# Attention kernel: projections in two halves after the scores, and the transposed maximum ahead of the last weighted values

## The chip, the cores and the metric

The kernel runs on one core of a Trainium2 chip. A core has TensorE (PE, matrix products; its weight loads are listed as PEld), VectorE (DVE), ScalarE (ACT), GpSimd (POOL) and SyncE (SP, which here only issues transfers). The metric is the time of one execution on the device in microseconds (us), the median of several runs.

## The reference, cut to what matters

32 batches of 128 tokens of width 128 go through cross attention with 16 heads and through a mixture of 8 experts of which each token takes 2.

```python
x = x + tanh(g_xattn[0]) * xattn(layernorm(x), ctx_1024, ctx_1024, ...)
x = x + tanh(g_ffn[0]) * ffn(layernorm(x), ...)

# xattn, with q the normalised x and k = v = the context
q, k = apply_rope(q), apply_rope(k)
Q, K, V = (split_heads(t @ W.T + b) for t, W, b in ...)     # 16 heads of 8
scores = einsum('bhqd,bhkd->bhqk', Q, K) / sqrt(8)
out = einsum('bhqk,bhkd->bhqd', softmax(scores), V)
return merge_heads(out) @ Wo_w.T + Wo_b

# ffn
xn = rms_norm(x, norm_scale)
c, ids = top-2 of softmax(xn @ w_router.T)
val, gate = split(xn @ w_up[e])                             # hidden width 352
out = sum over the two experts of c * ((val * silu(gate)) @ w_down[e]) + x
```

## The kernel before, in words

The program is written engine by engine: five instruction streams in fixed order, tied by semaphores that are counted. No scheduler moves anything, so an instruction runs when those ahead of it on its engine have gone and its semaphores have been reached. The attention part fills about 31 to 257 us of the profile, the expert part the rest.

The attention loop has one step a batch, b = 0 to 31. Four batches are a chunk c = b // 4, u = b % 4 is the place in it, and four steps are a period. Within step b TensorE does, for batch b, the scores by key (`scores_by_key`, L1348, four groups into the two banks STB), and the weighted values (`weighted_values`, L1361, four groups); for batch b+2, the scores by query (`scores`, L1335, four groups into the two banks SB); for batch b-1, the transposes of the heads (`heads_by_query`, L1388), of the attended rows (`transpose_attended`, L1399) and the output projection (`project_out`, L1403 and L1404). What softmax subtracts is found two steps ahead: DVE takes the maximum of each group of scores by query (`maximum`, L840, four a step), TensorE transposes them (`transpose_maximum`, L1393), and DVE writes them as a high part and a low part (`maximum_high` L847, `maximum_low` L851), which SP's transfers put below the stacked queries for `scores_by_key` of that batch. The transposed maximum lies in the bank of the second group of scores, so this group (L1335, g=1) of the next step waits until L851 has read it. ACT takes the exponent of each group of scores by key (L573), and copies the values' sums (`heads_out`, L580), the attended rows (L586) and others out of the banks.

On top of this each step does a part of what a whole chunk needs. In u=0: the V projection of chunk c+1 (L1321), the positions of routed rows (L1432 to L1435), on DVE the choice of experts and `shift` (L798). In u=1: the transposes of x (L1287) and of the context (L1295) for chunk c+2, their copies on ACT (L540, L547) and the rotation of Q on DVE (L806). In u=2: `project_q` (L1303, L1304) into the bank PR; ACT takes its high part in bf16 (`high`, L554), DVE the remainder (`remainder`, L832), ACT a middle part (L560), POOL the lowest; and `transpose_rows` (L1414) for the router of chunk c-1. In u=3: `project_k` (L1313, L1314) with the same parts, the router (L1423), and on ACT `base` (L602, four activations). Both projections, the V projection and all those transposes use the one bank PR in turn. POOL sends the routed rows out by indirect transfers (L427). SP's queue carries the stacked parts of Q and K (six pieces each a chunk), the maxima and the loads. Chunks 6 and 7 have no Q and K projection any more.

## Time and profile before

| | |
|---|---|
| median of 3 runs | 470.53 us (468.91 to 471.07) |
| the profiled execution | 470.41 us, its span 468.6 us |
| mean granted clock of TensorE | 0.917 of full speed |
| PE / DVE / ACT / POOL busy | 411.8 / 301.8 / 261.7 / 242.7 us |
| steps 12 to 15 (one period), 111.75 to 140.48 us | 28.73 us, PE busy 25.03 |

The profiled execution is 1.8 us longer than its span, since the span counts from the first to the last recorded instruction. A busy PE means matmuls in flight; their ends are modelled. What an engine waits for stands in brackets behind its row in the timeline, with the line that released it.

### The profile page before, as it was taken

How to read it: one execution, taken by the hardware profiler on the slowest of the kernel's cores; microseconds unless marked ns; L12 is line 12 of the kernel's file. 1: busy time of each engine (PE TensorE's matmuls, PEld its weight loads, DVE VectorE, ACT ScalarE, POOL GpSimd, SP SyncE). 2: the span in 40 equal slices, each digit the busy share in tenths (PEclk: the TensorE clock that was granted, in tenths of full speed). 3: DMA queues.
4: the chain of work that ended last, by engine and by line, in shares of the span. 5: the costliest groups of instructions: out<-in, count | busy, mean ns of one | idle time of the engine just before them, and what ended most of it. 6: DMA issues, size and time to landing. Idle time of an engine off the chain costs nothing.

```text
span 468.6 us, 13323 instructions
## 1 busy us (share of the span) xinstructions
PE 411.8 (88%) x3821; PEld 278.8 (59%) x3824; DVE 301.8 (64%) x1167; ACT 261.7 (56%) x582; POOL 242.7 (52%) x201
## 2 busy tenths in 40 slices
PE   7988899988898898989898939996799998999991
PEld 3445465645555466555555627674577876777871
DVE  6877888987878677777884414563655554555550
ACT  3437586977777676666665415752255554555540
POOL 6090242365446454454333475568466537886663
PEclk9998999999998897996956778998899999999997
DMA  7714341446579224232011322444334423344330
GB/s 185 177 47 126 75 112 35 121 135 173 145 206 232 63 65 115 77 88 79 30 43 48 87 52 43 68 59 94 59 48 61 58 47 49 56 57 56 37 28 0
DMA packets 57422, 39.07 MB, mean 83 GB/s; under 512 B 8819, under 2 KB 55158, under 8 KB 57366
## 3 DMA queue, kind: packets, MB, share of 16 engines
q1 hardware_dynamic: 43622, 28.87, 23.9%
q0 software_dynamic: 12736, 8.64, 13.1%
q10 hardware_dynamic: 1008, 0.85, 0.8%
q8 instruction: 30, 0.49, 0.5%
q14 instruction: 26, 0.21, 0.2%
HBM read 14.26 MB, written 11.75 MB: 56 GB/s over the span
## 4 chain that ended last, share of the span: by engine, by line
PE 61%; DVE 15%; issue 7%; ACT 5%; DMA 5%; another core or an unknown queue 4%; POOLq 1%; POOL 0%; DVEq 0%; ACTq 0%
PE bank L1595 9%; PE bank L1573 8%; PE bank L1575 7%; PE bank L1361 5%; DVE nmx L840 5%; PE bank L1585 4%; DMA out<-ys,yi 4%; PE bank L1388 3%; PE bank L1393 3%; PE bank L1335 3%; PE bank L1348 2%; PE bank L1303 2%; ACT pt L573 2%; PE bank L1304 2%
## 5 line engine op out<-in xcount | busy, mean ns | idle before, releaser
L509 POOL DMA_INDIRECT out<-ys,yi x72 | 112.6, 1564 | 63.8 <-issue 35.3
L427 POOL DMA_INDIRECT slots_dram<-xr,slu x64 | 62.7, 979 | 68.9 <-ACT pt L573 55.3
L840 DVE TENSOR_REDUCE nmx<-bank 128x4 f32<-128x512 f32 x128 | 81.8, 681 | 5.9 <-PE bank L1335 5.7
L1595 PEld LDWEIGHTS bank<-wf_sb,hT 128*128 128x128 f32 (+1 forms) x432 | 58.6, 197 | 39.0 <-issue 35.2
L1595 PE MATMUL bank<-wf_sb,hT 128*128 (+1 forms) x432 | 63.7, 285 | 19.9 <-DVE hT L1203 15.4
L573 ACT ACTIVATE pt<-bank 128x512 f32<-128x512 f32 x128 | 72.5, 594 | 14.6 <-PE bank L1348 12.8
L1193 DVE TENSOR_TENSOR hh<-sg,bank 128x352 f32<-128x352 f32 x72 | 37.5, 520 | 53.5 <-ACT sg L707 28.4
L715 ACT ACTIVATE ys<-bank,yc 128x128 f32<-128x128 f32 x72 | 26.5, 368 | 76.6 <-PE bank L1595 32.0
L1573 PE MATMUL bank<-wf_sb,xT 128*128 x144 | 58.1, 487 | 0.1
L1361 PE MATMUL bank<-pt,v 128*9 128x128 f32 x1024 | 53.7, 296 | 3.5 <-ACT pt L573 2.5
L1575 PE MATMUL bank<-wf_sb,xT 128*128 x144 | 55.9, 470 | 0.0
L1202 DVE COPY hT<-bank 128x256 f32<-128x256 f32 x72 | 30.5, 424 | 38.5 <-PE bank L1585 17.8
L1335 PE MATMUL bank<-ks,qs 62*128 62x128 bf16 x512 | 40.4, 229 | 8.4 <-DVE mTs L851 5.7
L707 ACT ACTIVATE sg<-bank 128x352 f32<-128x352 f32 x72 | 33.4, 464 | 17.2 <-PE bank L1573 10.3
L1575 PEld LDWEIGHTS bank<-wf_sb,xT 128*128 128x128 f32 x144 | 28.6, 199 | 16.6 <-issue 2.4
L1585 PE MATMUL bank<-con,hh 128*128 128x128 f32 (+1 forms) x216 | 36.6, 279 | 0.0
L1335 PEld LDWEIGHTS bank<-ks,qs 62*128 62x128 bf16 x512 | 28.0, 100 | 13.6 <-issue 9.2
L1361 PEld LDWEIGHTS bank<-pt,v 128*9 128x9 f32 x1024 | 16.7, 90 | 31.1 <-issue 17.4
L699 ACT ACTIVATE xT<-bank,ns_sb 128x128 f32<-128x128 f32 x72 | 26.4, 367 | 15.3 <-PE bank L1565 8.6
L1348 PE MATMUL bank<-qs,ks 64*128 64x128 bf16 x512 | 28.8, 235 | 0.0
L1388 PE MATMUL bank<-con,oT 128*128 128x128 f32 x128 | 24.8, 325 | 3.7 <-ACT oT L580 2.1
L408 POOL TENSOR_TENSOR parts<-r,parts 128x512 bf16<-128x512 f32 x14 | 16.2, 1161 | 22.5 <-ACT parts L560 22.3
(191 smaller groups left out, 699.9 us busy)
## 6 DMA issues: line engine op xcount, KB each, us to landing
qs<-parts SPq DMA_DIRECT2D x48, 128.0 KB
ks<-parts SPq DMA_DIRECT2D x45, 128.0 KB
xs<-slots_dram SPq DMA_DIRECT2D x72, 66.0 KB
wf_sb<-in_wup SPq DMA_DIRECT2D x8, 352.0 KB
x_sb<-in_x SPq DMA_DIRECT2D x8, 256.0 KB, 3.5
ctx_sb<-in_ctx_in SPq DMA_DIRECT2D x8, 256.0 KB, 3.7
out<-x_sb SPq DMA_DIRECT2D x8, 256.0 KB, 2.4
out<-ys,yi POOLq DMA_INDIRECT x72
```

The lines of the kernel that those rows point to most:

```text
L427: nc.gpsimd.indirect_dma_start(out=slots_dram, out_offset=bass.IndirectOffsetOnAxis(ap=slu[:, c % 2, k, kk:kk + 1], axis=0), in_=xr[:, c % ...
L509: nc.gpsimd.indirect_dma_start(out=out.rearrange("b s d -> (b s) d"), out_offset=bass.IndirectOffsetOnAxis(ap=yi[:, r:r + 1], axis=0), in_ ...
L573: nc.scalar.activation(pt[:, 4 * g:4 * g + 4, :], STB[g % 2][:, :].rearrange("p (h s) -> p h s", h=4), ACT.Exp, scale=SCORE_SCALE).then_in ...
L840: nc.vector.tensor_reduce(nmx[:, b % 2, at:at + 4], SB[g % 2][:, :].rearrange("p (h s) -> p h s", h=4), AX.X, ALU.max, negate=True).then_i ...
L1335: last = mm(SB[g % 2][:, k * S:(k + 1) * S], qs[row:row + ROWS, c % NST, i, t0:t0 + S], ks[row:row + ROWS, c % NST, i, t0:t0 + S], start=T ...
L1348: last = mm(STB[g % 2][:, k * S:(k + 1) * S], ks[row:row + 64, c % NST, i, t0:t0 + S], qs[row:row + 64, c % NST, i, t0:t0 + S], start=True ...
L1361: last = mm(PVB[32 * k:32 * k + DK + 1, g * S:(g + 1) * S], v9[:, c % 2, b % CH, 4 * g + k, :], pt[:, 4 * g + k, :], start=True, stop=True)
L1388: last = nc.tensor.transpose(HB[:, g * S:(g + 1) * S], oT[:, g, :], ident)
L1573: mm(bank[2 * (r % 2)][:, 0:H], xT[:, r % 2, :], wf_sb[:, bass.ds(w + H, H)], start=True, stop=True)\
L1575: mm(bank[2 * (r % 2) + 1][:, 0:H], xT[:, r % 2, :], wf_sb[:, bass.ds(w, H)], start=True, stop=True)\
L1585: last = nc.tensor.transpose(bank[5][0:w, 128 * n:128 * n + 128], hh[:, r % 2, 128 * n:128 * n + w], ident)
L1595: last = mm(Y[:, 0:D], hT[0:wide, r % 2, 128 * n:128 * n + 128], wf_sb[0:wide, bass.ds(w + 2 * H + n * D, D)], start=(n == 0), stop=(n == ...
```

## The change

Nothing is computed otherwise, and no instruction is added or dropped apart from waits. (1) TensorE: the projections of Q and K are cut into their two matmuls, which go behind the last scores of the step, with `transpose_attended` between them; this one and they come ahead of the second group of weighted values. (2) TensorE: `transpose_maximum` goes ahead of the third and fourth groups of weighted values, and ahead of the row transposes, the router and the context transposes. (3) ACT: the high part of Q goes from ahead of the third exponent to behind the fourth, that of K to the end of the step behind `base`. (4) DVE: the remainders go behind the transposed maximum's two parts; `shift` goes behind the choice of experts; `variance` goes between the third and fourth maximum and `widen` ahead of the parts. (5) The row transposes of chunks 0 to 5 use the bank HB in place of PR, with waits to match. The diff, cut to its core:

```diff
@@ act @@
-                if u == 2 and there(c + 2):
-                    high(c + 2, 0, PR)
-                if u == 3 and there(c + 2):
-                    high(c + 2, 1, PR)
...
                     rows(c - 1, (2, 3))
+                if u == 2 and there(c + 2):
+                    high(c + 2, 0, PR)
                 if u == 2 and there(c - 1) and c < NCH - 1:
                     rows_transposed(c - 1)
...
                 if u == 3 and there(c - 1):
                     base(c - 1)
+                if u == 3 and there(c + 2):
+                    high(c + 2, 1, PR)
@@ dve @@
-                if u == 0 and there(c + 2) and c:
-                    shift(c + 2)
...
-                if u == 2 and there(c + 2):
-                    remainder(c + 2, 0, PR)
-                if u == 3 and there(c + 2):
-                    remainder(c + 2, 1, PR)
...
                     choose_sum(c - 2)
+                if u == 0 and there(c + 2) and c:
+                    shift(c + 2)
                 if real(b + 2):
                     maximum(b + 2, 2)
+                if u == 3 and there(c + 3):
+                    variance(c + 3)
                 if real(b + 2):
                     maximum(b + 2, 3)
...
                 if u == 3 and there(c + 3):
-                    variance(c + 3)
+                    widen(c + 3)
                 if real(b + 2):
                     maximum_high(b + 2)
                     maximum_low(b + 2)
+                if u == 2 and there(c + 2):
+                    remainder(c + 2, 0, PR)
+                if u == 3 and there(c + 2):
+                    remainder(c + 2, 1, PR)
@@ pe @@
-            def project_q(n, ps):
+            def project_q(n, ps, half):
 
-                pe.wait_ge(d_q, n + 1)
-                if n >= 2:
-                    pe.wait_ge(a_cT, n + 1)
-                mm(ps[:, :], wqk_sb[:, 0, :], qa[:, :], start=True, stop=False)
-                mm(ps[:, :], wqk_sb[:, 1, :], qb[:, :], start=False, stop=True).then_inc(pe_q, 1)
+                if half == 0:
+                    pe.wait_ge(d_q, n + 1)
+                    if n >= 2:
+                        pe.wait_ge(a_cT, n + 1)
+                    mm(ps[:, :], wqk_sb[:, 0, :], qa[:, :], start=True, stop=False)
+                else:
+                    mm(ps[:, :], wqk_sb[:, 1, :], qb[:, :], start=False, stop=True).then_inc(pe_q, 1)
...
@@ heads_by_query @@
+                if u == 2 and there(c - 1) and c < NCH - 1:
+                    pe.wait_ge(a_nT, c)
@@ transpose_rows @@
-                if c == NCH - 1:
-                    pe.wait_ge(d_tp, c)
-                pe.wait_ge(d_rq, min(c + 4, NCH))
-                pe.wait_ge(d_rk, min(c + 3, NCH))
-                pe.wait_ge(a_v, min(c + 3, NCH))
+                if c == NCH - 2:
+                    pe.wait_ge(a_v, NCH)
+                else:
+                    pe.wait_ge(d_on, min(b, B))
+                    if c:
+                        pe.wait_ge(d_tp, c)
@@ the loop of pe @@
-                if u == 2 and there(c + 2):
-                    project_q(c + 2, PR)
-                if u == 3 and there(c + 2):
-                    project_k(c + 2, PR)
...
                     scores(b + 2, 3)
+                if u == 2 and there(c + 2):
+                    project_q(c + 2, PR, 0)
+                if u == 3 and there(c + 2):
+                    project_k(c + 2, PR, 0)
+                if real(b - 1):
+                    transpose_attended(b - 1)
+                if u == 2 and there(c + 2):
+                    project_q(c + 2, PR, 1)
+                if u == 3 and there(c + 2):
+                    project_k(c + 2, PR, 1)
                 if real(b):
                     weighted_values(b, 1)
-                if real(b - 1):
-                    transpose_attended(b - 1)
...
+                if real(b + 2):
+                    transpose_maximum(b + 2)
+                if u == 2 and there(c - 1) and c < NCH - 1:
+                    transpose_rows(c - 1, b)
+                if u == 3 and there(c - 1) and c < NCH - 1:
+                    router(c - 1, b)
+                if u == 1 and there(c + 2):
+                    transposes_ctx(c + 2, PR)
...
                 if real(b):
                     weighted_values(b, 2)
                     weighted_values(b, 3)
-                if real(b + 2):
-                    transpose_maximum(b + 2)
```

TensorE in step u=3 of the second chunk, before: from the heads' transposes (out of `oT`) over the projection of K (`ka`, `kb`), the values (`pt,v`), the scores by key (`qs,ks`) and by query (`ks,qs`) and the router (`nTs`) to the transposed maximum (`nmx`) and the output projection (`onT`).

```order
132 L1388 MATMUL bank<-con,oT 128x128 x4
133 L1313 MATMUL bank<-ka,wqk_sb 128x512
134 L1314 MATMUL bank<-kb,wqk_sb 128x512
135 L1361 MATMUL bank<-pt,v 9x128 x4
136 L1348 MATMUL bank<-qs,ks 128x128 x8
137 L1335 MATMUL bank<-ks,qs 128x128 x8
138 L1361 MATMUL bank<-pt,v 9x128 x4
139 L1399 MATMUL bank<-con,on 128x128
140 L1423 MATMUL bank<-wr_sb,nTs 128x8 x4
141 L1361 MATMUL bank<-pt,v 9x128 x8
142 L1393 MATMUL bank<-con,nmx 16x128
143 L1403 MATMUL bank<-wo_sb,onT 128x128
```

The same place of TensorE in the changed kernel.

```order
133 L1392 MATMUL bank<-con,oT 128x128 x4
134 L1363 MATMUL bank<-pt,v 9x128 x4
135 L1350 MATMUL bank<-qs,ks 128x128 x8
136 L1337 MATMUL bank<-ks,qs 128x128 x8
137 L1314 MATMUL bank<-ka,wqk_sb 128x512
138 L1403 MATMUL bank<-con,on 128x128
139 L1316 MATMUL bank<-kb,wqk_sb 128x512
140 L1363 MATMUL bank<-pt,v 9x128 x4
141 L1397 MATMUL bank<-con,nmx 16x128
142 L1428 MATMUL bank<-wr_sb,nTs 128x8 x4
143 L1363 MATMUL bank<-pt,v 9x128 x8
144 L1407 MATMUL bank<-wo_sb,onT 128x128
```

The projection's two matmuls have gone behind the scores, with the attended transpose between them, and the transposed maximum has passed the router and eight value matmuls.

VectorE in the third chunk's step u=3 and on into the next, before: remainder (`r`), maxima (`nmx`), variance (`BN_AGGR`), the two parts of the transposed maximum (`mTs`), router scores (`sc`), attention added (`x_sb`), then step u=0.

```order
188 L832 SCALAR_TENSOR_TENSOR r<-bank,bqk_sb,parts 128x512
189 L840 TENSOR_REDUCE nmx<-bank 128x4 x2
190 L789 BN_AGGR mv<-st 128x2 x4
191 L847 CAST mTs<-bank 16x128
192 L851 TENSOR_TENSOR mTs<-bank,mTs 16x128
193 L903 COPY sc<-bank 128x32
194 L868 SCALAR_TENSOR_TENSOR x_sb<-bank,tg,x_sb 128x128
195 L794 TENSOR_SCALAR ve<-mv 128x4
196 L874 BN_STATS st6b<-x_sb 128x6
197 L840 TENSOR_REDUCE nmx<-bank 128x4 x2
```

VectorE in the changed kernel, at the same place.

```order
190 L840 TENSOR_REDUCE nmx<-bank 128x4
191 L789 BN_AGGR mv<-st 128x2 x4
192 L840 TENSOR_REDUCE nmx<-bank 128x4
193 L794 TENSOR_SCALAR ve<-mv 128x4
194 L847 CAST mTs<-bank 16x128
195 L851 TENSOR_TENSOR mTs<-bank,mTs 16x128
196 L832 SCALAR_TENSOR_TENSOR r<-bank,bqk_sb,parts 128x512
197 L903 COPY sc<-bank 128x32
198 L868 SCALAR_TENSOR_TENSOR x_sb<-bank,tg,x_sb 128x128
199 L874 BN_STATS st6b<-x_sb 128x6
```

The remainder now stands behind both parts of the transposed maximum, and the variance between two maxima.

ScalarE in the fifth chunk's step u=3 and the start of the next, before: exponents (`pt`), the K high part (`parts<-bank`), attended rows (`onT`), the middle part (`parts<-r`), base rows (`x_sb`) and the heads' copy (`oT`).

```order
170 L573 ACTIVATE pt<-bank 128x512 x2
171 L554 ACTIVATE parts<-bank,bqk_sb 128x512
172 L573 ACTIVATE pt<-bank 128x512
173 L586 ACTIVATE onT<-bank 128x128
174 L573 ACTIVATE pt<-bank 128x512
175 L560 ACTIVATE parts<-r 128x512
176 L602 ACTIVATE x_sb<-x_sb,fbias,fscale 128x128 x4
177 L580 ACTIVATE oT<-bank 128x512
```

ScalarE at the same place in the changed kernel.

```order
165 L573 ACTIVATE pt<-bank 128x512 x3
166 L586 ACTIVATE onT<-bank 128x128
167 L573 ACTIVATE pt<-bank 128x512
168 L560 ACTIVATE parts<-r 128x512
169 L602 ACTIVATE x_sb<-x_sb,fbias,fscale 128x128 x4
170 L554 ACTIVATE parts<-bank,bqk_sb 128x512
171 L580 ACTIVATE oT<-bank 128x512
```

The K high part has moved from behind the second exponent to the end of the step, between the base rows and the next step's copy of the heads.

## Rows read from the trace of the kernel before

**Rows 1.** The page: granted clock of TensorE in 40 slices, tenths of full speed

```profile
PEclk9998999999998897996956778998899999999997
```

**Rows 2.** Windows: stretch, its length, busy us (x instructions) by engine, PEclk, DMA share, GB/s

```profile
111.75:119.17 7.42, 5.70 (x97) 4.04 (x96) 6.09 (x28) 6.62 (x16) 5.49 (x6) 1.00 0.71 175
119.17:125.86 6.69, 5.67 (x83) 3.61 (x82) 5.75 (x29) 4.52 (x10) 2.71 (x2) 1.00 0.57 158
125.86:133.92 8.06, 7.10 (x83) 3.69 (x82) 6.96 (x18) 5.90 (x12) 5.16 (x5) 1.00 0.59 169
133.92:140.48 6.56, 6.56 (x87) 4.20 (x86) 4.71 (x14) 4.30 (x10) 2.07 (x3) 1.00 0.63 176
178.62:186.65 8.03, 7.85 (x83) 5.25 (x82) 6.12 (x30) 4.66 (x10) 3.64 (x3) 0.57 0.36 95
```

**Rows 3.** Waits of PE from 38 to 257 us: total us, times, longest

```profile
PE bank L1335 <- DVE mTs L851: 4.9, 7, 1.4
```

**Rows 4.** Line 847 by itself: DVE idle before it until this releaser, us, times

```profile
  PE bank L1393: 18.8, 23
```

**Rows 5.** Timeline, steps 12 and 13: start us, length us, engine, line, operation

```profile
115.08 0.85 DVE L798 SCALAR_TENSOR_TENSOR nmr<-mv,rs 128x4 f32<-128x4 f32 x1
...
117.24 1.28 DVE L840 TENSOR_REDUCE nmx<-bank 128x4 f32<-128x512 f32 x2
...
118.58 0.28 PE L1393 MATMUL bank<-con,nmx 128*16 128x128 f32 x1
...
119.54 0.28 DVE L847 CAST mTs<-bank 16x128 bf16<-16x128 f32 x1 [1.02 <-PE bank L1393]
...
120.16 0.33 DVE L868 SCALAR_TENSOR_TENSOR x_sb<-bank,tg,x_sb 128x128 f32<-128x128 f32 x1
...
121.42 1.28 DVE L840 TENSOR_REDUCE nmx<-bank 128x4 f32<-128x512 f32 x2
```

**Rows 6.** Timeline, from step 13 into step 14

```profile
123.82 1.28 DVE L840 TENSOR_REDUCE nmx<-bank 128x4 f32<-128x512 f32 x2
123.91 0.60 PE L1295 MATMUL bank<-con,ctx_sb 128*128 128x128 f32 x4
...
124.77 0.60 ACT L547 ACTIVATE cTs<-bank 128x512 f32<-128x512 f32 x1
...
125.27 0.28 PE L1393 MATMUL bank<-con,nmx 128*16 128x128 f32 x1
...
126.22 0.60 ACT L580 ACTIVATE oT<-bank 128x512 f32<-128x512 f32 x1
...
127.20 0.66 PE L1388 MATMUL bank<-con,oT 128*128 128x128 f32 x4
```

**Rows 7.** Timeline, step 15 and the start of step 16

```profile
137.16 0.69 ACT L554 ACTIVATE parts<-bank,bqk_sb 128x512 bf16<-128x512 f32 x1 [1.50 <-PE bank L1314]
...
137.88 0.75 DVE L832 SCALAR_TENSOR_TENSOR r<-bank,bqk_sb,parts 128x512 f32<-128x512 f32 x1 [1.32 <-ACT parts L554]
...
138.24 0.33 PE L1399 MATMUL bank<-con,on 128*128 128x128 f32 x1
...
139.29 0.62 PE L1361 MATMUL bank<-pt,v 128*9 128x128 f32 x16
...
139.77 1.64 ACT L602 ACTIVATE x_sb<-x_sb,fbias,fscale 128x128 f32<-128x128 f32 x4
...
139.88 0.28 PE L1393 MATMUL bank<-con,nmx 128*16 128x128 f32 x1
...
142.41 1.27 DVE L840 TENSOR_REDUCE nmx<-bank 128x4 f32<-128x512 f32 x2
```

**Rows 8.** Timeline, step 27

```profile
225.13 1.29 DVE L840 TENSOR_REDUCE nmx<-bank 128x4 f32<-128x512 f32 x2
...
226.79 0.28 PE L1393 MATMUL bank<-con,nmx 128*16 128x128 f32 x1
...
227.23 0.28 DVE L847 CAST mTs<-bank 16x128 bf16<-16x128 f32 x1 [0.82 <-PE bank L1393]
```

51 lines of the change are left out of this document (24 added, 27 removed).

## The prediction

> **What bounds the kernel now.** I read the page first, then windows one step long, then PE's waits, then the timeline at the hand-overs that the change touches. The change acts on the 32 attention steps (about 31 to 257 us); the expert part behind them keeps its order and only starts earlier or later. Four steps make a period, because the projections, rows and routing of a chunk of four batches are spread over four steps. In one steady period the windows [rows 2] show two kinds of step. Steps 14 and 15 (the ones that hold the Q and the K projection) are TensorE's: PE is busy 7.10 of 8.06 and 6.56 of 6.56 us. Steps 12 and 13 belong to VectorE: PE is busy only 5.70 of 7.42 and 5.67 of 6.69 us, and DVE does 6.09 and 5.75 us of work that PE has to wait for. The reader is to see that the period has 28.73 us and PE 25.03 us of work, so at most 3.70 us a period could go, and only if DVE and ACT deliver in time.
>
> The named stall is at L1335: the second group of scores may not overwrite the bank that holds the transposed maximum until L851 has read it. It costs 4.9 us, in 7 places [rows 3]. Ahead of it lies the hand-over from the transposed maximum (L1393) to DVE's L847, on which DVE idles 18.8 us in 23 places [rows 4]. From start to start it takes 0.44 us in step 27 [rows 8] and 0.96 us in step 12 [rows 5]. The Trainium skill (Perfetto Trace Analysis, Summary: the profiler window per engine type) says that a matmul's end is estimated and that the travel of its semaphore is not shown; by that, these gaps are real hand-over time that moves along with the instruction, and the trace, where no row explains the 0.96, agrees. The sum below takes both gaps as ends.
>
> **The change, part by part, on the period of rows 5 to 7.** No instruction is added or taken away: only order and waits change, so everything is a matter of who is late.
>
> *Shift behind the routing (step 12).* L798 took 0.85 us here though it is a 128x4 operation [rows 5]; it ran beside a POOL operation. Moved to just ahead of the third maximum it should cost 0.10 to 0.85; I take 0.4, since POOL's work no longer meets it but can meet a neighbour. The third maximum then starts 0.4 earlier than 117.24, and the transposed maximum, which stands directly behind the fourth, comes at 118.2 instead of 118.58.
>
> *Transposed maximum ahead of the last values (every step).* PE waits there for DVE's fourth maximum, and what was ahead of it as cover is now behind. In step 12 nothing is lost by waiting (PE waited there before), but the last two weighted values (0.59, the distance from L1361 at 139.29 to L1393 at 139.88 [rows 7]) and the output projection (with the transpose 0.59: L1393 at 118.58 to the end of step 12 at 119.17 [rows 2, 5]) come behind: step 12 ends at 118.2+0.59+0.59 = 119.4, 0.2 late. DVE gains: L847 can start at 118.6 to 119.2 instead of 119.54, and then has to wait for the output projection at L868, which needs the end of step 12 plus a hand-over: 119.5 to 119.8 instead of 120.16. The next maxima follow L868 by 1.26 as before: 120.8 to 121.1 instead of 121.42. The stall at L1335 is gone here.
>
> In step 13 the bill comes [rows 6]. The transposed maximum follows the fourth maximum, as far behind the first pair as now (123.82+1.28 = 125.10 against 121.42, 3.68), so at 124.5 to 124.8 against 125.27. Behind it now stand the transposes of the context (0.53, from L1295 at 123.91 to the next matmul), the values 0.59 and the projection: step 13 ends at 126.2 to 126.5, against 125.86: 0.3 to 0.6 late. ACT's copy of the context (L547) moves from 124.77 to 125.2 to 125.5, and with it the rows and L580, from 126.22 to 126.65 to 126.95. L580 takes 0.60 us and L1388 needs it: 127.3 to 127.6, against 127.20.
>
> *Projection of Q after the scores, in halves (step 14).* From L1388 at 127.20 to its end at 133.92 step 14 took 6.72 us. PE was idle 0.96 us of the whole step [rows 2]; I put 0.3 of it to the stall at L1335 ahead of L1388 (the mean of those in [rows 3] is 0.7) and 0.66 behind it: for the rotated Q, for the bank at L1414 that the remainder had to leave, for the last exponents. With the projection between scores and values these waits shrink, because DVE and ACT work under it: 6.06 to 6.36 us remain. Step 14 ends at 127.3+6.06 = 133.4 at best and 127.6+6.36 = 134.0 at worst, against 133.92; middle 0.25 early. The attended transpose between the halves waits for nothing, and it frees ACT earlier. The remainder of Q behind the mask of maxima on DVE is hidden under the output projection.
>
> *Projection of K (step 15).* PE was full, 6.56 of 6.56 [rows 2], and stays full. So step 15 keeps its length. What could make the next step late is ACT: the high part of K (L554, 0.69) no longer goes ahead of the third exponent but behind the base rows (L602, 1.64), and the K remainder, the copy of router scores, L868 and the first maxima of step 16 are queued behind it on DVE; PE waits for it with the V projection. But the attended transpose, for which ACT waited at 138.24, now runs before the second half of the projection, about 1.5 us earlier, so L602 starts at about 138.3 instead of 139.77. Then 138.3+1.64+0.69 = 140.6 for the high part, and remainder, copy, L868 and statistics (0.75 of L832 [rows 7], 0.33 of L868 [rows 5], and some 0.35 for the copy and a statistics operation, an estimate by the size of L868) put the first maximum of step 16 at 142.0 to 142.1, against 142.41 [rows 7]. The gain of step 14 passes through, no more. On SP's queue the three K pieces and, behind them, the maxima of step 16 wait for that high part; it comes 2.8 us later than the 137.85 of now, but those maxima are only made at the end of step 16, so nobody waits for it.
>
> *Sum.* A steady period gains 0.3 us; ends: +0.2 (lost) with the slow ends of each chain, -0.9 with the fast ones. There are four (chunks 2 to 5): -1.2. In the two periods before them DVE has no routing, nothing stalls at L1335, and the 0.3 to 0.6 us of step 13 falls on a full PE: I charge +0.15 each, +0.3. At the end, steps without projection have nothing to put under the wait. Step 27 [rows 8]: the fourth maximum ends at 226.42. L1393 stands at 226.79; without the values (0.59) and the router (L1399 to L1361 is 1.05 [rows 7], some 0.2 of it the transpose that stays ahead) PE would arrive at 225.35 and wait 1.07. The next step then starts up to 1.1 later and the maximum of step 28 about 0.6. Part of that is won back where TensorE is at half clock and slower than DVE. I charge +0.5. Together -0.4 on the profiled execution's 470.41: 470.0. The median of the runs is 0.12 above that execution, which changes nothing.
>
> *The clock.* It is the term that the rows bound worst. The granted clock falls in the second half of the attention part [rows 1]; step 21, at a mean of 0.57, took 8.03 us, where step 13, the same work at 1.00, took 6.69 [rows 2]: 1.34 us for one fall. The falls follow steps of the VectorE kind. The change leaves the PE idle time there about as it is (less at L1335, more at L1393), so I take 0, with two falls more or fewer as ends: ±2.7. The Trainium skill (TensorE: Matmul & The Clock Gate, Part 1: The HAM clock gate) ties the lower clock to stretches in which the engine idles; by that alone there would be no fall in the attention part, and this term would be 0 for certain. The trace does not agree: no VectorE step of [rows 2] at full clock has PE idle for more than a quarter of its time, and the clock falls among steps like these.
>
> **Rivals.** *Faster, about 465.5.* The stalls at L1335 are the true limit and go without a bill: -4.9 us [rows 3] give 465.5; with a shorter L798 and one fall of the clock less it could be 463. For it: DVE idles 18.8 us at that hand-over [rows 4], and in the VectorE steps each tenth counts. Against: L868 waits for the output projection, which I have behind two more groups of values.
> *Slower, about 474.* PE queues in order, and at the early transposed maximum router, context transposes, values and output projection stand behind DVE's fourth maximum. Price up to 1.07 us a step [rows 8]; it decides as soon as DVE's fourth maximum ends later than PE has done its scores and the first values, which can be so in the 18 steps that have a maximum to transpose and no projection of Q or K. With 1.07 us not won back in two or three of them (+2.7) and one fall of the clock more (+1.34): 474.4. Against: in the steady period DVE gets its input earlier for it.
> *The move does nothing.* The K remainder hangs on ACT's base rows, as worked out; if L602 does not start earlier, the high part ends at 142.1 and step 16 begins 1.2 us late each period, which eats the 0.3: 470 to 474, shared between my forecast and the slower case.
>
> **How the numbers follow.** My forecast (470.0, own range 468.2 to 472.5) gets 0.43, the faster rival 0.34, the slower one with the K remainder 0.23. A change of 0.5%, 2.35 us, is about what a measurement of this kernel can tell from none. The range: four periods between +0.2 and -0.9, the clock ±2.7 and the ends' 1 us, opened to the faster rival's 465.5 and to 474: 464.5 to 474. Faster by over 0.5%: 0.35, the faster rival and a sliver of mine; slower: 0.22; within: 0.43.
>
> **What would show it.** Right: no wait of PE at the second scores for the mask of maxima; a new PE or weight-load wait at the transposed maximum for DVE's maximum, 0.5 to 1 us in steps without a projection; steps 14 and 15 at 7.0 to 7.4 and 6.5 us from heads to heads; the K high part just behind the base rows; DVE's idle time ahead of L847 down to some 8 us. Wrong: VectorE steps shorter than 6.4 us (faster rival); step 13 over 7.2 us or the clock at half in chunk 2 or 3 (slower rival); a first maximum of step 16 that starts later after its step's beginning than 1.9 us (the K remainder).

## The result: 1.3 % slower, and the profile after

The changed kernel takes 476.52 us (median of 4 runs, 472.14 to 477.44) against 470.43 us (4 runs, 468.91 to 471.07): ratio 1.013, 95 % interval 1.008 to 1.018. The forecast was 470.0 with a range to 474.0: the measured time is 6.5 us above the one and 2.5 above the other. Two later groups of runs, each with its own runs of the kernel before, gave 1.014 (1.011 to 1.018) and 1.022 (1.019 to 1.026) for the same kernel. Medians are over all executions of a kernel, while ratios leave out those more than 1.5 % above its fastest; that matters most for late_in_last, where it is 5 of 12. The profiled execution took 475.71 us with a span of 473.9 us, 5.3 us over the span before.

Line numbers behind the change are a little higher: the transposed maximum is L1397 (was L1393), project_out L1407 and L1408, the scores L1337, the heads L1392, the attended transpose L1403; VectorE's and ScalarE's lines keep their numbers.

The granted clock, to be laid beside [rows 1]:

```profile
PEclk9987999999898997977755587999599999999997
```

Windows of steps 12, 13, 14 and 15, then the six steps 24 to 29 of chunks 6 and 7 that have a maximum to transpose, then the last three. Columns as in [rows 2]:

```profile
112.47:119.98 7.51, 5.57 (x97) 3.90 (x96) 6.30 (x29) 5.89 (x14) 4.27 (x5) 1.00 0.73 176
119.98:127.19 7.21, 6.43 (x82) 4.40 (x81) 6.60 (x30) 4.41 (x9) 3.66 (x3) 0.76 0.46 124
127.19:134.10 6.91, 6.43 (x82) 3.69 (x82) 5.96 (x16) 5.98 (x13) 4.46 (x4) 1.00 0.69 196
134.10:140.95 6.85, 6.85 (x86) 4.25 (x86) 4.38 (x15) 5.16 (x12) 2.96 (x3) 1.00 0.76 213
199.73:246.34 46.61, 38.85 (x496) 23.96 (x495) 33.01 (x140) 25.82 (x54) 16.26 (x16) 0.71 0.18 50
246.34:268.99 22.65, 20.00 (x155) 12.12 (x155) 10.21 (x68) 11.74 (x26) 5.74 (x6) 0.50 0.29 75
```

The same two stretches at the end in the kernel before:

```profile
200.54:240.76 40.22, 36.42 (x496) 22.46 (x495) 31.46 (x134) 25.57 (x55) 17.14 (x17) 0.78 0.21 60
240.76:262.63 21.87, 19.18 (x156) 11.54 (x155) 11.51 (x75) 12.26 (x27) 6.31 (x7) 0.58 0.25 71
```

This locates the loss in this pair of executions. Up to the end of step 23 the changed kernel is 0.8 us ahead (199.73 against 200.54). The six steps 24 to 29 lose 6.4 us, the last three 0.8, and the expert part gives 1.1 back (204.9 against 206.0): +5.3 together. In the period of steps 12 to 15, Q is 1.15 us shorter than in [rows 2], but the other three are longer by 0.09, 0.52 and 0.29 us.

What TensorE and VectorE waited for in the attention part of the changed kernel, from 38 to 265 us (total, times, longest):

```profile
PE bank L1397 <- DVE nmx L840: 12.2, 18, 0.9
DVE x_sb L868 <- PE bank L1408: 13.1, 18, 1.7
DVE mTs L847 <- PE bank L1397: 11.1, 18, 1.0
```

The stall of [rows 3] is gone, as announced. In its place TensorE stands 12.2 us at the transposed maximum. VectorE idles less ahead of L847 (11.1 against 18.4 us, its wait by the same view before), but 13.1 us at L868 for project_out, a wait that the kernel before has only in its very last step: the two together have grown from 18.4 to 24.2 us. Timeline of the changed kernel, step 26 and its end (starts in the first column):

```profile
218.33 1.28 DVE L840 TENSOR_REDUCE nmx<-bank 128x4 f32<-128x512 f32 x2
219.67 0.38 PE L1397 MATMUL bank<-con,nmx 128*16 128x128 f32 x1 [0.53 <-DVE nmx L840]
219.84 1.06 PE L1419 MATMUL bank<-con,xr 128*128 128x128 f32 x4
221.72 0.26 PE L1450 MATMUL bank<-conb,carry 128*8 128x1 bf16 x5 [0.82 <-issue]
221.88 1.01 PE L1363 MATMUL bank<-pt,v 128*9 128x128 f32 x13
223.54 0.28 PE L1408 MATMUL bank<-bop,conb 3*128 3x128 bf16 x1
223.87 0.35 DVE L868 SCALAR_TENSOR_TENSOR x_sb<-bank,tg,x_sb 128x128 f32<-128x128 f32 x1 [1.24 <-PE bank L1408]
224.83 1.29 DVE L840 TENSOR_REDUCE nmx<-bank 128x4 f32<-128x512 f32 x2 [0.28 <-PE bank L1337]
```

One loop stands in these rows. The fourth maximum ends at 219.61 (218.33 and 1.28), and only then may TensorE go on; rows, counts, values and project_out follow in its queue until 223.54; VectorE, 1.24 us idle, adds the result at 223.87 and only behind that begins the maxima of the next step, at whose end TensorE stands again. Each engine waits for the other once a step; from the end of that maximum to the last matmul of project_out it is 3.9 us.

Step 26 is the longest case. In the mean of steps 24 to 29 this stretch takes 2.3 us (1.2 to 3.9), in the kernel before 1.0 (0.5 to 1.4). And 0.82 us of the 3.9 aren't the maximum's: count_rows (L1450) writes the bank into which part 5 of the change has put the row transposes, and has to wait for ScalarE's copy of them, which ends at 221.63. The kernel before has no such wait. It comes once, and every run made from the changed kernel has it, with the maximum late too.

### The profile page after: what moved, and what is told of

Read it like the earlier page. It is cut to its first block, busy times and chain, and to the rows that moved or that the text cites. A ratio compares the mean times of both kernels' runs of the same rounds, so it can differ in the third digit from the quotient of the medians.

```text
span 473.9 us, 13316 instructions
## 1 busy us (share of the span) xinstructions
PE 414.8 (88%) x3821; PEld 282.9 (60%) x3824; DVE 301.9 (64%) x1167; ACT 263.4 (56%) x582; POOL 245.8 (52%) x201
## 4 chain that ended last, share of the span: by engine, by line
PE 65%; DVE 18%; issue 6%; ACT 5%; another core or an unknown queue 3%; DMA 1%; POOLq 0%; POOL 0%; DVEq 0%; ACTq 0%
PE bank L1609 11%; PE bank L1587 9%; PE bank L1589 9%; DVE nmx L840 9%; PE bank L1363 6%; PE bank L1599 5%; PE bank L1392 3%; PE bank L1350 3%; PE bank L1407 3%; PE bank L1337 2%; PE bank L1304 2%; ACT x_sb L602 2%; PE bank L1579 2%; PE bank L1397 2%
## 5 line engine op out<-in xcount | busy, mean ns | idle before, releaser
L427 POOL DMA_INDIRECT slots_dram<-xr,slu x64 | 65.5, 1023 | 70.8 <-ACT pt L573 56.4
L1202 DVE COPY hT<-bank 128x256 f32<-128x256 f32 x72 | 30.5, 424 | 38.1 <-PE bank L1599 18.4
L1363 PE MATMUL bank<-pt,v 128*9 128x128 f32 x1024 | 52.4, 306 | 0.4 <-ACT pt L573 0.4
L1337 PE MATMUL bank<-ks,qs 62*128 62x128 bf16 x512 | 35.0, 235 | 1.2 <-DVE nmx L840 0.5
L1363 PEld LDWEIGHTS bank<-pt,v 128*9 128x9 f32 x1024 | 19.6, 93 | 24.2 <-issue 19.7
L1392 PE MATMUL bank<-con,oT 128*128 128x128 f32 x128 | 25.8, 335 | 6.9 <-DVE sc L903 2.8
L1350 PE MATMUL bank<-qs,ks 64*128 64x128 bf16 x512 | 30.1, 241 | 0.0
L414 POOL TENSOR_TENSOR rs<-ve,mhalf 128x8 f32<-128x8 f32 x8 | 13.3, 1662 | 31.9 <-DVE ve L886 31.9
```

The source lines that it names most:

```text
L427: nc.gpsimd.indirect_dma_start(out=slots_dram, out_offset=bass.IndirectOffsetOnAxis(ap=slu[:, c % 2, k, kk:kk + 1], axis=0), in_=xr[:, c % ...
L1337: last = mm(SB[g % 2][:, k * S:(k + 1) * S], qs[row:row + ROWS, c % NST, i, t0:t0 + S], ks[row:row + ROWS, c % NST, i, t0:t0 + S], start=T ...
L1350: last = mm(STB[g % 2][:, k * S:(k + 1) * S], ks[row:row + 64, c % NST, i, t0:t0 + S], qs[row:row + 64, c % NST, i, t0:t0 + S], start=True ...
L1363: last = mm(PVB[32 * k:32 * k + DK + 1, g * S:(g + 1) * S], v9[:, c % 2, b % CH, 4 * g + k, :], pt[:, 4 * g + k, :], start=True, stop=True)
L1392: last = nc.tensor.transpose(HB[:, g * S:(g + 1) * S], oT[:, g, :], ident)
```

## The experiments

Steps are told by what they hold: R (routing, as step 12), C (transposes of the context, step 13), Q and K (steps 14 and 15). Ratios are to the kernel before on the same chip. A step's length is that of a window from project_out to project_out.

**The transposed maximum late again, and the transposed maximum alone.** tmax_late undoes one half of the change, tmax_only does that half alone in the kernel before.

```
 tmax_late:                                  tmax_only (in the kernel before):
-    transpose_maximum(b + 2)                    transpose_attended(b - 1)
     ...                                         (router, positions of the last chunks)
     weighted_values(b, 3)                  +    transpose_maximum(b + 2)
+    transpose_maximum(b + 2)                    (context, rows, router, counts)
     project_out(b - 1)                          weighted_values(b, 2) ... (b, 3)
                                            -    transpose_maximum(b + 2)
```

> The changed kernel with one part undone: the transposed maximum again behind the last weighted values, projections and all else as changed. Theory A (the loss is the transposed maximum's early place: PE waits there for the fourth maximum, 12.2 us in 18 places, and the output projection behind it makes DVE wait at L868, 13.1 us in 18): about 4 to 7 us faster than the changed kernel's 476.5, so 469.5 to 472.5. Theory B (the loss comes from the moved projections and remainders, which make the K steps 6.85 us in place of 6.56 and leave step u=0 late): stays at 475 to 477. Theory C (neither, the clock of TensorE happened to be low in the last two chunks): 474 to 477 with the same two chunks slow.

> The kernel before with one part of the change alone: the transposed maximum ahead of the context and row transposes, the router and the last weighted values. Theory A: slower than before by 4 to 8 us (474.5 to 478.5), since the steps with a projection lose their cover too: the projection stands ahead of the scores there. Theory B: 469 to 471.5. Theory C: 470 to 474, if the clock falls more often.

tmax_late: 482.78 us, ratio 1.033 (1.027 to 1.039). tmax_only: 491.6 us, 1.048 (1.042 to 1.053). Alone, the two halves cost 2.6 and 3.7 times the 1.3 % of both together, so the parts can't be priced one by one. With the maximum late and the projections behind the scores, VectorE waits for it everywhere:

```profile
DVE mTs L847 <- PE bank L1397: 47.4, 30, 4.5
```

K steps take 7.68 us and Q steps 8.85 at full clock (6.85 and 6.75 in the changed kernel). With the early maximum alone TensorE stands in 29 of the steps, those with a projection too:

```profile
PE bank L1393 <- DVE nmx L840: 28.6, 29, 1.6
DVE x_sb L868 <- PE bank L1404: 19.6, 23, 2.0
```

The projections behind the scores are the cover for the early maximum in Q and K steps. The steps without a projection have no such cover.

**project_out first.** If VectorE's wait at L868 matters, project_out directly behind the transposed maximum shortens it.

```
     transpose_maximum(b + 2)
+    project_out(b - 1)
     ...
     weighted_values(b, 3)
-    project_out(b - 1)
```

> The changed kernel, with the output projection of batch b-1 directly behind the transposed maximum, ahead of row and context transposes, router and the last values. It separates the two waits inside theory A. If the wait of DVE at L868 for the output projection is what costs (A1), it comes down from 13.1 us to under 3, DVE reaches the next maxima 0.5 us earlier in each of 18 steps, and the time is 466 to 471. If PE's own standing at the transposed maximum costs (A2), the time stays at 474 to 477. Theory B: 475 to 477.

Measured 472.08 us, ratio 1.010 (1.006 to 1.013), against 1.013 and 1.014 of the changed kernel, which did not run on this chip. The wait at L868 fell to 3.9 us in 2 places, but the last values now end later, and with them ScalarE's copy of them, for which the heads wait:

```profile
PE bank L1392 <- ACT oT L580: 12.9, 16, 3.3
```

It was 1.6 us in 4 places in the changed kernel. R steps grew to 8.15 us and Q steps to 7.28, C steps shrank to 6.53. A wait was mostly exchanged for another.

**Late only where no projection is.** late_in_last has the maximum late in chunks 6 and 7 alone; tmax_early_proj has it late in all 18 steps without a projection; early_proj_sc moves the K high part and the copy of router scores forward as well.

```
     if real(b + 2) and EARLY:
         transpose_maximum(b + 2)
     ...
     weighted_values(b, 3)
+    if real(b + 2) and not EARLY:
+        transpose_maximum(b + 2)
 late_in_last:      EARLY = there(c + 2)
 tmax_early_proj:   EARLY = u >= 2 and there(c + 2)
```

> The changed kernel with the transposed maximum at its old place in chunks 6 and 7 only, where there is no projection (the 7 us were lost there: step 23 to the end of step 31 took 69.3 us against 62.1). Theory A: most of the loss goes, 469.5 to 472.5. Theory B: no gain, since chunks 6 and 7 have no Q or K projection in either kernel but were slow all the same: 475 to 477. Theory C (clock by chance): 474 to 477.

> The changed kernel with the transposed maximum early only in the 12 steps with a Q or K projection, and at its old place, behind the last values and the row and context transposes, in the other 18. Theory A: all of the loss goes and the gain of the Q steps (8.06 to 6.91 us) stays: 0.5 to 1.5% faster than before, 461 to 466 on a chip where before takes 468. Theory B: no better than the changed kernel. A theory D, that step u=0 and u=1 of chunks 2 to 5 gain from the early place (DVE sees it sooner) and only chunks 6 and 7 lose, expects it slower than the version that is late in chunks 6 and 7 only (ratio 1.003 to before).

> As the one with the transposed maximum early in the projection steps only, and besides ACT takes the high part of K ahead of the middle part and the base rows, and DVE copies the router scores ahead of the K remainder. In the changed kernel PE waits 2.8 us in 5 places at the heads' transposes for that copy. If the K remainder behind ACT's base rows is a part of the loss, step u=0 gets 0.3 to 0.5 us shorter and the time falls by 1 to 2 us against the same version without it; if step u=0 is bound by the choice of experts on DVE, within 0.5 us.

late_in_last: 471.32 us, 1.003 (0.999 to 1.008). Its median over that of the kernel before is 1.007, so between half of the loss and most of it comes back; the changed kernel did not run on this chip. tmax_early_proj: 477.42 us, 1.014 (1.010 to 1.019): R steps 6.79 and C steps 6.62 us at full clock are indeed shorter (7.5 and 6.9 in the changed kernel), but the Q steps behind them explode, one at full clock and one not:

```profile
159.78:168.67 8.89, 7.12 (x82) 3.96 (x82) 7.15 (x19) 6.12 (x13) 5.40 (x5) 1.00 0.21 62
127.15:139.33 12.18, 10.15 (x83) 5.01 (x82) 7.15 (x19) 6.14 (x13) 5.11 (x5) 0.72 0.41 117
```

The second scores of the Q step wait again for the bank with the transposed maximum of the C step (2.7 us in 5 places), and everything behind them, the projection's halves and the attended transpose, moves with them. In those C steps (9, 13, 17, 21) it takes 1.39 to 1.75 us from the start of L1397 to the start of L847, where most steps have 0.31 (tmax_late has 1.40 to 1.54 in the same steps). No trace from the two chips on which the kernel before takes 438 to 439 us has more than 0.42 there, so what this order would cost on them is open. early_proj_sc: 479.76 us, 1.016 (1.011 to 1.022); no gain.

**The clock.** warm_fill puts two matmuls of 512 columns into TensorE's stand in steps 25 to 29; after_again is the changed kernel on the same chip.

```
+    if (c == NCH - 2 and u) or (c == NCH - 1 and u < 2):
+        pe.wait_ge(a_v, NCH)
+        keep_warm(PR, 2)
     transpose_maximum(b + 2)
```

> The changed kernel once more, word for word, beside the others of this group on one chip. Any theory: 1.008 to 1.018 of the time of before. Theory A (early transposed maximum without cover) expects its profile to show the extra time against before in steps without a Q or K projection, and a gain in the Q steps; theory C (the clock, by chance) expects chunks 6 and 7 to be slow in some executions only.

> The changed kernel with two more matmuls of 512 columns (on a table of ones, into a bank that nobody reads then) ahead of the transposed maximum in steps 25 to 29, where PE waits for the fourth maximum anyway. They lie in the wait, so they cost about nothing; they only keep PE at work. If the half clock of chunks 6 and 7 is a result of these waits (A3), the clock stays at full for more of it and the time falls by 2 to 4 us against the changed kernel. If the waits themselves are the price and the clock only an addition by chance, the time stays within 1 us or rises by up to 1.

after_again 476.7 us, 1.014 (1.011 to 1.018); warm_fill 474.56 us, 1.010 (1.006 to 1.014). In the profiled executions the six steps took 40.85 us at a mean clock of 0.96, against 43.22 at 0.81. Work without any use in the stand saves 2.1 us: part of the loss is the lower clock. The mean granted clock of whole executions says the same: 0.889 to 0.903 in the six of after_again, 0.910 to 0.928 in the six of warm_fill, 0.914 to 0.934 in the kernel before on that chip.

**One term by itself.** last_only is the kernel before with the early maximum in chunks 6 and 7 and nowhere else. short_max is the changed kernel with the fourth maximum there taken over 16 of 128 keys, so only its duration changes. both_fixes and late_u0_last are candidates.

```
 short_max:
+    k = 16 if g == 3 and b >= CH * (NCH - 2) + 2 else S
     nc.vector.tensor_reduce(nmx[...], SB[g % 2][...][:, :, 0:k], ...)
 late_u0_last:  EARLY = not (u == 0 or not there(c + 2))
 both_fixes:    EARLY = there(c + 2), and project_out(b - 1) behind it there
```

> The kernel before, with one thing of the change only: in the eight steps of chunks 6 and 7 (of which six have maxima to transpose) the transposed maximum stands ahead of the row transposes, the router, the row counts and the last two weighted values; chunks 0 to 5 and the projections stay as before. Queue theory (TensorE stands for the fourth maximum there and everything behind it waits, project_out and with it VectorE's add_attention): steps 24 to 31 take about 67 to 69 us in place of 62, so 475 us, ratio 1.010 to 1.015, with the waits L1393 <- nmx and L868 <- project_out appearing in those steps alone. Rival (the loss of the changed kernel in chunks 6 and 7 comes with what chunks 0 to 5 hand over, or with the order of weighted_values(1) and the attended transpose, not with the early maximum): within 0.3 % of before.

> The changed kernel, but the fourth group of maxima in the steps of chunks 6 and 7 reduces 16 of the 128 columns (the maximum over the other keys is left out there); order and waits are unchanged. The wait named is that of TensorE for VectorE's fourth maximum (0.65 us long), with VectorE late. Queue theory: each of the six steps with a maximum ends about 0.45 us earlier, TensorE's wait at L1397 in these steps falls from 0.9 to about 0.5: 473 to 474.5, ratio 1.006 to 1.009. Rival (the bound there is a chain through the scores, the exponents and the values that does not pass the fourth maximum): 476 to 477, ratio 1.013.

> The changed kernel with the transposed maximum late in chunks 6 and 7 and, in chunks 0 to 5, project_out directly behind the early transposed maximum. Late in the last chunks gave back 1.0 % of the changed kernel's time (471.3) and project_out first 0.5 to 0.9 % (472.1). If the two losses lie in different steps they add up: 467.5 to 469.5, ratio 0.993 to 1.000. If project_out first gained only in chunks 6 and 7 (same loss counted twice): 471 to 472.5, ratio 1.003.

> The changed kernel with the transposed maximum behind the last weighted values in the first step (u = 0) of each chunk and in chunks 6 and 7, early in all others. Queue theory: steps with u = 0 go from 7.5 to about 6.8 us, and steps with u = 1, 2 and 3 keep their length (6.9 to 7.2, 6.8, 6.85), since the maximum that their scores need is early again: six times 0.6 us below late_in_last (471.3), so 467 to 469, ratio 0.995 to 1.000. Rival (the loss is only handed on: the row after a late maximum gets longer by what the step gained, as the Q step did when u = 1 was late): u = 1 steps at 7.5 and more, 471 to 473, ratio 1.003.

last_only: 444.29 us, 1.011 (1.008 to 1.015), the ratio and the waits that were expected: 4.9 us on a chip where before takes 439.35. On that same chip steps 24 to 29 take 41.61 us, against 37.76 in late_u0_last:

```profile
PE bank L1393 <- DVE nmx L840: 4.3, 6, 1.1
DVE x_sb L868 <- PE bank L1404: 4.4, 5, 1.3
```

late_u0_last 440.06 us, 1.001 (0.997 to 1.005); both_fixes 443.12, 1.010 (1.007 to 1.013), so the gains of its two parts don't add up: its R steps take 8.30 us at full clock. short_max gave 445.19, 1.015 (1.010 to 1.019), which by its text speaks for the rival, but the changed kernel itself was not run on that chip.

**The same, with the control on the chip.** whole_k is late_u0_again with both halves of the K projection behind the attended transpose.

```
-    project_k(c + 2, PR, 0)
     transpose_attended(b - 1)
+    project_k(c + 2, PR, 0)
     project_k(c + 2, PR, 1)
```

> The changed kernel itself, as the control for the other three: ratio 1.011 to 1.016 to before.

> The changed kernel with the fourth group of maxima in chunks 6 and 7 reduced over 16 of 128 columns (the maximum over the other keys is left out there). Queue theory: the steps with a maximum in chunks 6 and 7 no longer wait at L1397 and take 3 us less together than those of after_third; time 0.993 of after_third. Rival (the bound is a chain that doesn't pass the fourth maximum): within 0.2 % of after_third and the same length of chunks 6 and 7.

> The changed kernel with the transposed maximum late in the first step of each chunk and in chunks 6 and 7, once more. If what it gives back is all that the changed kernel lost: 0.997 to 1.003 of before, and 0.985 to 0.99 of the changed kernel on this chip. If the pattern with both halves early and late is better than before where the clock is not halved: 0.990 to 0.997.

> late_u0_again with the K projection whole again: both halves behind the attended transpose, none ahead of it. If the split costs the 0.29 us (TensorE changes between tiles of 512 and of 128 columns once more, and is the bound of the K step, 6.84 us busy of 6.84): K steps at 6.5 to 6.6, six times 0.25 us, 1.5 us and 0.3 % below late_u0_again. Rival (the 0.29 us are the early transposed maximum and the swap of rows around it, or the router): K steps at 6.8 to 6.9 and no change.

before 438.1 us; after_third 448.03, 1.022 (1.019 to 1.026); short_max_again 444.26, 1.015 (1.010 to 1.019); late_u0_again 440.75, 1.004 (1.001 to 1.007); whole_k 438.26, 1.000 (0.997 to 1.002). short_max_again is 3.8 us below its control, 0.992 where 0.993 was expected, and its steps 24 to 29 take 36.70 us against 40.47. So in chunks 6 and 7 the steps hang on the fourth maximum; the first short_max was only read against the wrong control. It doesn't show that the stand is the price, since the shorter maximum also takes VectorE 0.47 us less in each of six steps (0.21 in place of 0.68): its 36.70 us are 2.3 below the 39.0 of late_u0_again, whose maximum is late there and whole. For the early place itself last_only is the test.

late_u0_again is 7.3 us below after_third. In the two profiled executions nearly all of it lies ahead of step 24: 6.7 us in steps 8 to 23, 1.7 before them, 0.2 from step 24 to the last. Windows of one period (steps R, C, Q, K), first of after_third, then of late_u0_again:

```profile
114.54:122.89 8.35, 6.41 (x97) 4.21 (x96) 6.30 (x29) 6.62 (x15) 4.27 (x5) 0.87 0.75 172
122.89:130.57 7.68, 6.91 (x83) 4.74 (x82) 6.57 (x30) 3.92 (x9) 3.66 (x3) 0.70 0.38 110
130.57:137.32 6.75, 6.30 (x83) 3.56 (x82) 5.95 (x16) 5.94 (x13) 4.46 (x4) 1.00 0.70 200
137.32:144.16 6.84, 6.84 (x86) 4.24 (x85) 4.38 (x15) 5.06 (x12) 2.96 (x3) 1.00 0.72 189
```

```profile
111.18:117.94 6.76, 5.38 (x97) 3.82 (x96) 5.76 (x27) 6.02 (x15) 4.27 (x5) 1.00 0.85 198
117.94:125.06 7.12, 5.59 (x82) 3.78 (x82) 6.91 (x33) 4.38 (x9) 3.38 (x3) 1.00 0.45 128
125.06:131.81 6.75, 6.30 (x83) 3.57 (x82) 5.96 (x16) 5.94 (x13) 5.77 (x5) 1.00 0.69 191
131.81:138.66 6.85, 6.85 (x87) 4.26 (x86) 4.38 (x15) 5.06 (x12) 2.97 (x3) 1.00 0.79 217
```

Q and K steps agree to 0.01 us. The R step is 0.75 us shorter at full clock (7.50 elsewhere in the changed kernel), and the clock no longer falls in it or in the C step behind it: with the fall, 1.59 and 0.56 us. At full clock the C step is longer than the changed kernel's (7.12 against 6.91).

whole_k was right in its price and wrong in its place. The K step became longer (7.04), the R step behind it shorter by more, 5.92 against 6.75:

```profile
132.71:139.75 7.04, 6.88 (x86) 4.26 (x85) 4.89 (x16) 5.66 (x13) 3.82 (x4) 1.00 0.77 214
139.75:145.67 5.92, 5.27 (x97) 3.82 (x96) 5.27 (x27) 5.47 (x14) 3.41 (x4) 1.00 1.10 217
```

K and R together take 12.96 us against 13.60. Neither the split as a bound of the K step nor the rival had this: the attended transpose is earlier, so what ScalarE owes to the K remainder and the next first maxima is earlier too.

**A version that beats both.** ctx_first is whole_k with the context transposes ahead of the early maximum in C steps, as work for the stand; ctx_first_whole_q has the Q projection whole too.

```
+    if u == 1 and there(c + 2): transposes_ctx(c + 2, PR)
     transpose_maximum(b + 2)
-    if u == 1 and there(c + 2): transposes_ctx(c + 2, PR)
```

> whole_k, with the four transposes of the context (0.66 us of TensorE) ahead of the early transposed maximum in the step u = 1, not behind it. If the stand there is empty time for TensorE and the maximum is what it waits for: the wait at L1397 in these six steps goes from 0.5 to 0.8 us to 0.1 or less, u = 1 steps from 7.12 to about 6.6, six times 0.5 us, so 0.993 of whole_k and 0.990 to 0.997 of before. Rival (VectorE sets the step, 6.9 us busy of 7.12, and not TensorE): steps u = 1 at 7.0 to 7.1 and 0.998 to 1.002 of before.

> ctx_first with the Q projection whole too, both halves behind the attended transpose. If its split costs what that of K did (0.4 to 0.65 us per chunk in the step or the one behind): another 0.5 % below ctx_first. Rival (the Q step is bound by VectorE and ScalarE, 5.95 us each of 6.75, and the K step behind it by TensorE): Q and K steps as in ctx_first, no change.

ctx_first: 465.12 us against 468.39, ratio 0.992 (0.988 to 0.995), faster than the kernel before by more than its interval, in one group of runs. ctx_first_whole_q: 466.82 us, 0.997 (0.993 to 1.000); a whole Q projection gives nothing (Q steps 7.33 against 7.06). The reason given for ctx_first did not hold. The stand did go (0.2 us in one place between 100 and 200 us, 2.6 in 5 for whole_k), but its C steps take 7.23 us, not 6.6, and Q steps 7.06 in place of 6.75. Its trace has the clock at 1.00 in every one of steps 8 to 23:

```profile
PEclk9998999999999999997876879998899999999997
```

That execution is the fastest of the eleven, though, with a mean clock of 0.946; the others have 0.916 to 0.937, the kernel before on that chip 0.909 to 0.945. So the clock isn't shown as the reason for the 0.8 %. It ran on another chip than whole_k, so how much of the difference of their ratios is the edit's stays open.

## Why the prediction was wrong

Mean length of the windows of steps 8 to 23 whose granted clock is 1.00 (number of windows), the length of all sixteen, and of steps 24 to 29, from one execution each:

| order | R | C | Q | K | steps 8 to 23 | steps 24 to 29 |
|---|---|---|---|---|---|---|
| as before (its own trace) | 7.22 (4) | 6.36 (2) | 7.91 (3) | 6.56 (4) | 116.2 | 40.2 |
| as changed (its own trace) | 7.49 (3) | 6.91 (1) | 6.80 (3) | 6.89 (4) | 115.3 | 46.6 |
| as before (last_only) | 7.11 (3) | 6.04 (3) | 7.50 (4) | 6.56 (4) | 109.5 | 41.6 (early there) |
| as changed (short_max_again) | 7.47 (2) | 6.91 (1) | 6.75 (4) | 6.85 (4) | 114.2 | 36.7 (short maximum) |
| as changed (after_third) | 7.44 (1) | none | 6.75 (3) | 6.84 (4) | 117.7 | 40.5 |
| late_u0_again | 6.73 (4) | 7.12 (3) | 6.75 (3) | 6.85 (4) | 111.0 | 39.0 |
| whole_k | 5.90 (4) | 7.12 (2) | 6.75 (2) | 7.04 (4) | 110.6 | 37.7 |
| ctx_first | 6.18 (4) | 7.23 (4) | 7.06 (4) | 7.22 (4) | 110.8 | 39.7 |

The first two rows, the profiled pair, are at 28.05 and 28.09 us a period, the next two, from the two faster chips, at 27.21 and 27.98. So at full clock the new order loses nothing against the one execution of the old order and 0.8 us against the other. The changed kernel's steps are nearly the same on all chips; the old order's are not, and the next point says in what they differ.

- *Bound and stall.* Right that R and C steps are VectorE's, and that the stall at L1335 goes. Wrong in what its going is worth: the wait moved to L1397 and L868 and grew. The stall is also no fixed property of the old order. last_only has the old order in chunks 0 to 5, and from 38 to 265 us it has no wait of TensorE at L1335 for L851. The prediction called the 0.96 us from L1393 to L847 a hand-over time that moves along with the instruction. The kernel before's own execution has 0.88 to 1.82 us in ten of steps 4 to 29; the changed kernel at most 0.66, last_only at most 0.42. Step 13 of before and the same place in last_only, then last_only's waits, to be laid beside [rows 4]:

```profile
126.15 0.28 DVE L847 CAST mTs<-bank 16x128 bf16<-16x128 f32 x1 [0.72 <-PE bank L1393]
126.44 0.28 PE L1393 MATMUL bank<-con,nmx 128*16 128x128 f32 x1
126.75 0.28 DVE L847 CAST mTs<-bank 16x128 bf16<-16x128 f32 x1
DVE mTs L847 <- PE bank L1393: 7.6, 15, 1.0
```

  With L1393 at 125.27 [rows 6], that is 0.88 against 0.31 us. What makes the long ones is open. VectorE's idle time ahead of L847 came to 11.1 us, not to some 8.
- *Step 12 (R), "0.2 late".* Right in this period (+0.09) and at full clock in the later ones (7.51 against 7.40 in last_only); step 8 alone is 0.9 late (7.44 against 6.52), which makes most of the 0.36 between the means. L798 fell from 0.85 to 0.16 us, more than the 0.4 taken:

```profile
117.38 0.16 DVE L798 SCALAR_TENSOR_TENSOR nmr<-mv,rs 128x4 f32<-128x4 f32 x1
118.80 0.28 PE L1397 MATMUL bank<-con,nmx 128*16 128x128 f32 x1 [0.77 <-DVE nmx L840]
120.24 0.35 DVE L868 SCALAR_TENSOR_TENSOR x_sb<-bank,tg,x_sb 128x128 f32<-128x128 f32 x1 [0.44 <-PE bank L1408]
```

  L1397 starts 6.33 us after its step's beginning (118.80 less 112.47), where L1393 stood 6.98 after it (118.58 less 111.60, the last matmul of project_out there): 0.65 us won, and 0.75 lost behind it (1.18 us to the step's end against 0.43).
- *Step 13 (C), "0.3 to 0.6 late".* +0.52 in this period, in the range, at a clock of 0.76; at full clock +0.87 on the means of the two faster chips (one step against three). The sign of a step over 7.2 us was met (7.21), the sign that the prediction gave to the slower rival.
- *Step 14 (Q), "0.25 early".* Right in kind and too low in size: 0.75 us by the means of the faster chips, 1.11 by the profiled pair's. It was set against a Q step of 8.06 us, and at full clock those of the old order take 7.43 to 8.18, so how much its gain outweighs the rest depends on the execution that was read.
- *Step 15 (K), "keeps its length".* Wrong, +0.29. TensorE is full in it (6.85 of 6.85), so it is more of TensorE's time in the new order; whole_k shows that the split half costs K and R together 0.64 us. What was feared of ScalarE did not come: the high part follows the base rows 0.36 us ahead of the step's end (140.95), and the first maximum of step 16 starts 1.70 us behind it, where before it was 2.09 (142.41 less 140.32), so the third rival is out:

```profile
140.59 0.67 ACT L554 ACTIVATE parts<-bank,bqk_sb 128x512 bf16<-128x512 f32 x1
142.65 1.27 DVE L840 TENSOR_REDUCE nmx<-bank 128x4 f32<-128x512 f32 x2
```

- *The sum over the periods, "-1.2 + 0.3".* In the profiled pair the changed kernel is 0.8 us ahead at the end of step 23, where -0.9 was forecast. It is a hit for this pair and partly luck: before's execution had the long hand-overs and a step of 10.10 us at a clock of 0.83 in that stretch. On the faster chips steps 8 to 23 took 109.5 us in the old order (last_only), 114.2 and 117.7 in the new, each in one execution.
- *The end, "+0.5".* The step that failed most: +0.5 us was charged for all steps without projection at the end, and steps 24 to 29 alone lost 6.4 in the profiled pair. The wait per step was put at 1.07 us and measured 0.6 in the mean and 0.9 at most (3.6 us in 6 steps); but the prediction let most of it be won back, and it is not: last_only, with the early maximum in chunks 6 and 7 as its only change, costs 4.9 us, 1.1 %. The loop through L868 was left out. VectorE's next maxima stand behind project_out, which stands behind the wait for this step's maximum, so a delay returns each step in place of being absorbed.
- *The clock, "0, ±2.7".* Taken as independent of the change; it is tied to it. On each of the two chips with a control, the executions of the changed kernel have a lower mean clock than those of the kernel before (0.889 to 0.903 against 0.914 to 0.934, 0.928 to 0.945 against 0.945 to 0.970). In the changed order the falls begin in R and C steps, in which TensorE stands at L1397, and with the maximum late in R steps nearly all of them between steps 8 and 23 are gone (late_u0_again, after_third: 1 and 4 stretches). The Trainium skill (TensorE: Matmul & The Clock Gate, Part 1: The HAM clock gate) ties the lower clock to idle stretches; the direction agrees with late_u0_again and warm_fill, though no wait at L1397 is longer than 0.9 us.

The slower rival (474.4) named the mechanism: TensorE's queue standing at the early maximum, in the 18 steps without a projection, and a fall of the clock more. The wait was seen in exactly 18 places. It charged two or three steps where nearly all pay, and its 474.4 lay outside the range that was stated.

What stays open: where the loss lies on a given chip (in the profiled pair it is in steps 24 to 29, between after_third and late_u0_again in steps 8 to 23), why the falls differ in place and number between executions of one kernel, and what TensorE does in the additional 0.29 us of a K step.

## What to carry to other kernels

A wait that is moved forward in an in-order queue needs cover in each kind of step, and steps without that cover have to be priced one by one; here late in every uncovered step gave 1.014, no better than early everywhere, because the Q step behind each late C step grew; late in the R steps and in the last two chunks gave 1.001 and 1.004. Where two engines each wait for the other once a step, follow the loop round: a delay comes back in the next step and is not won back. Read more than one period, and if there is one a second execution, and compare windows of equal granted clock, before a period's length is taken as the base.

## What the runs showed of the hardware

The time of the same kernel before differs by chip: medians of 470.2, 468.2 and 468.4 us on three, 439.4 and 438.1 on two others. The granted clock goes with it (0.92 to 0.93 against 0.96). On the one of the two faster chips where the changed kernel ran, its ratio was worse, 1.022 against 1.013 and 1.014; one chip doesn't show that the clock is the reason.

A fall of the clock can cost far more than the 1.34 us of [rows 2]: two Q steps of tmax_early_proj took 12.18 us at a mean of 0.72 and 8.89 at 1.00, 3.3 us more, with VectorE's work at 7.15 us in both and TensorE busy 10.15 and 7.12 us.

The time from the start of the transposed maximum to the start of the VectorE instruction that reads it was 0.31 us in most steps of every trace. Between steps 4 and 29, eight of the twelve traces in whose group the kernel before takes 468 to 470 us have steps with 0.8 to 2.0; in the eight traces from the two faster chips it never passes 0.42.

Two matmuls of no use in TensorE's stand, in each of five steps, made the kernel faster (warm_fill, 0.4 %).
